# Taking the next tile's rows before a tile's last gelus, in a routed feed-forward stage on one NeuronCore

## The reference, cut to what matters

```
gate = softmax(xt @ Wg);  topv, topi = top_k(gate, 2);  scores[t, topi] = topv / (sum(topv) + 1e-6)
for e in range(8):
    h = gelu(xt @ W1[e] + b1[e])        # 256 -> 1024, exact gelu
    ye = h @ W2[e] + b2[e]              # 1024 -> 256
    out = out + ye * scores[:, e:e + 1]
```

## Time and profile before

| | us |
|---|---|
| median of 3 runs | 413.33 (411.07 to 414.03) |
| profiled execution | 412.78 |
| its span, first to last instruction | 410.8 |
| TensorE matmuls busy | 370.0 (90%) |
| VectorE busy | 259.3 (63%) |
| ScalarE busy | 255.5 (62%) |
| GpSimd busy | 179.0 (44%) |

### The profile page before, as it was taken

The page is one execution under the profiler, slowest core; times in us unless marked ns, Lnnn a source line. Parts: engine busy times, 40 slices in busy tenths (PEclk is TensorE's granted clock), DMA queues, the critical chain, the costliest instruction groups (busy, mean ns, idle before and its releaser), DMA issues.

```text
span 410.8 us, 8335 instructions
## 1 busy us (share of the span) xinstructions
PE 370.0 (90%) x2574; PEld 334.0 (81%) x2575; DVE 259.3 (63%) x651; ACT 255.5 (62%) x554; POOL 179.0 (44%) x227
## 2 busy tenths in 40 slices
PE   5989969999999997999989999999999999999950
PEld 4535557887888886999989899899999999899950
DVE  5868487796867876565467446784467754935530
ACT  2587556678658941756557566786567855765520
POOL 5800000002024544335655556675657546766553
PEclk9799999999999787999999999999999999999985
DMA  8810000000020781718224841569324624242342
GB/s 262 267 38 2 0 1 2 0 2 0 2 75 30 310 306 44 246 28 253 56 56 71 225 65 41 141 165 260 56 50 105 191 41 72 34 67 52 53 61 29
DMA packets 22964, 38.61 MB, mean 94 GB/s; under 512 B 2576, under 2 KB 17296, under 8 KB 22800
## 3 DMA queue, kind: packets, MB, share of 16 engines
q0 software_dynamic: 8032, 12.82, 18.7%
q1 hardware_dynamic: 14896, 25.41, 17.9%
HBM read 28.85 MB, written 9.37 MB: 93 GB/s over the span
## 4 chain that ended last, share of the span: by engine, by line
PE 39%; issue 7%; POOL 5%; DMA 5%; DVE 2%; ACT 2%; POOLq 1%; DVEq 0%; ACTq 0%
PE banks L1253 6%; PE banks L1577 6%; PE banks L1579 6%; PE banks L1581 6%; PE banks L1255 6%; PE banks L1254 6%; DMA xg<-xn_rows,idx_in 5%; PE banks L1554 3%; POOL xg L519 2%; POOL out_rows L565 2%; DVE y_out L1193 1%; ACT h_raw L812 0%; ACT h_hi L815 0%; ACT x_hi L802 0%; DVE w_lo L1211 0%
## 5 line engine op out<-in xcount | busy, mean ns | idle before, releaser
L812 ACT ACTIVATE h_raw<-banks,b1t 128x256 f32<-128x256 f32 (+1 forms) x136 | 68.0, 500 | 75.8 <-PE banks L1255 70.5
L1202 DVE TENSOR_TENSOR h_lo<-h_raw,h_hi 128x256 fp32r<-128x256 f32 (+1 forms) x136 | 59.8, 444 | 67.3 <-ACT h_hi L815 51.5
L565 POOL DMA_INDIRECT out_rows<-y_out,idx_out x36 | 68.6, 1907 | 42.8 <-DVE y_out L1193 37.0
L1253 PE MATMUL banks<-x_hi,w_hi 128*128 128x256 f32 (+1 forms) x272 | 79.6, 293 | 6.5 <-issue 3.9
L1577 PE MATMUL banks<-w_hi,h_hi 128*128 128x256 f32 x288 | 83.3, 289 | 1.0 <-DVE h_lo L1202 1.0
L1581 PE MATMUL banks<-w_hi,h_lo 128*128 128x256 f32 x288 | 81.4, 283 | 0.0
L1579 PE MATMUL banks<-w_lo,h_hi 128*128 128x256 f32 x288 | 81.4, 283 | 0.0
L1254 PE MATMUL banks<-x_lo,w_hi 128*128 128x256 f32 (+1 forms) x272 | 78.6, 289 | 0.0
L1255 PE MATMUL banks<-x_hi,w_lo 128*128 128x256 f32 (+1 forms) x272 | 78.6, 289 | 0.0
L519 POOL DMA_INDIRECT xg<-xn_rows,idx_in x57 | 58.0, 1017 | 27.8 <-POOL idx_in L514 16.2
L815 ACT ACTIVATE h_hi<-banks,b1t 128x256 fp32r<-128x256 f32 (+1 forms) x136 | 67.9, 499 | 0.0
(11 more groups left out here) (212 smaller groups left out, 676.1 us busy)
## 6 DMA issues: line engine op xcount, KB each, us to landing
w_raw<-in_w SPq DMA_DIRECT2D x16, 1024.0 KB
xn_rows<-xn SPq DMA_DIRECT2D x2, 1056.0 KB, 4.8
x<-in_x_tok SPq DMA_DIRECT2D x4, 512.0 KB, 5.6
out_rows<-x SPq DMA_DIRECT2D x1, 2048.0 KB, 9.3
b2b<-in_b SPq DMA_DIRECT2D x1, 1024.0 KB, 5.0
xg<-xn_rows,idx_in POOLq DMA_INDIRECT x57
out_rows<-y_out,idx_out POOLq DMA_INDIRECT x36, 3.9
out_rows<-x POOLq DMA_DIRECT2D x1, 384.0 KB, 3.2
```

What stands on the lines that cost most here:

```text
L565: pool.indirect_dma_start(out_d, bass.IndirectOffsetOnAxis(ap=idx_out[:, i:i + 1], axis=0), y_out[:, i, :], None, compute_op=ALU.add).then ...
L812: act.activation(h_raw[j % RING][:, 0:w], banks[:, j % RING, 0:w], ACT.Gelu, bias=bias)
L1202: dve.tensor_tensor(h_lo[:, j, 0:w], h_raw[j % RING][:, 0:w], h_hi[:, j, 0:w].bitcast(F32), ALU.subtract).then_inc(h_split, 1)
L1253: pe.matmul(out, a_hi, b_hi, start=start, stop=False)
```

## The change

On ScalarE, `x_high(t + 1)` goes from behind the last pair of gelus to ahead of it: behind the wait for the tile's last group of layer 1 and ahead of the wait for h_split. This holds in tiles with and without weight pieces. On VectorE, `x_low(t + 1)` goes from behind the last h_lo (and from ahead of the last w_lo, where there is one) to ahead of the waits for the last h_lo. No instruction is added or taken away.

```diff
@@ ScalarE, tile
                 for j in range(HJ):
                     act.wait_ge(l1_ready, t * HJ + (j + 1))
+                    if j == HJ - 1:
+
+                        x_high(t + 1)
 
                     act.wait_ge(h_split, t * HJ + (j + 1))
...
                         c = slice(j * PIECE, (j + 1) * PIECE)
-                        if j == HJ - 1:
-                            x_high(t + 1)
                         act.activation(w_hi[(e + 1) % 2][:, c], w_raw[(e + 1) % 2][:, c], ACT.Copy
                                        ).then_inc(whi_done, 1)
-                if not (split and e + 1 < E):
-                    x_high(t + 1)
@@ VectorE, tile
                 for j in range(HJ):
+                    if j == HJ - 1:
+                        x_low(t + 1)
                     dve.wait_ge(gelu_done, t * HJ + (j + 1 + RING))
                     dve.wait_ge(l2_done, t * HJ + (j + 1))
                     dve.tensor_tensor(h_lo[:, j, 0:w], h_raw[j % RING][:, 0:w], h_hi[:, j, 0:w].bitcast(F32),
...
                         c = slice(j * PIECE, (j + 1) * PIECE)
-                        if j == HJ - 1:
-                            x_low(t + 1)
                         dve.wait_ge(whi_done, HJ * (e + 1) + j + 1)
...
-                if not (split and e + 1 < E):
-                    x_low(t + 1)
```

## The result

The changed kernel takes 426.77 us (median of 4 runs, 425.92 to 427.34) against 412.72 us before (median of 4 runs): a ratio of 1.033, 95% interval 1.028 to 1.038. It is slower by 14 us. The forecast was 423.0 in a range of 416.5 to 427.0, slower with a chance of 0.85.

What follows compares the result with a forecast made beforehand. TensorE's order of instructions was taken as the bound. Ends inside an expert (2.8 us) and changes of expert (4.9 after tiles 2, 5, 9, 12; 2.5 after 6, 10, 13) gave +10.2 on 412.8: 423 us, range 416.5 to 427.

Steps and rivals of the forecast that it cites:

- The shift of the last h_lo: After a two-block tile without weight pieces, the last h_lo ends 1.50 us later, in tile 1 at 195.76 instead of 194.26.
- Inside an expert: Seven ends of two-block tiles: next start 0.65 us later each, 4.55 us together, of which 2.8 stay.
- At a change of expert: Next start 2.35 us after the last h_lo: 1.28 us later after tiles 2, 5, 9, 12, and 0.84 after 6, 10, 13.
- The clock: Rival: longer TensorE gaps lower the granted clock in the expert stage, some 8 us more, 431 us; chance 0.03.
- The rival of a gain: Starts after a change of expert wait for x_lo or the last w_lo; x_lo gains 2.5 us, 410.3 us; chance 0.06.
- the stalls at L1574: Sign: TensorE's layer 2 waits for h_lo grow from 3 places to about 15 and from 1.0 to 4 us.
- ScalarE's idle time before x_hi: Sign: in two-block tiles without weight pieces, ScalarE idles about 0.6 us before x_hi instead of before h_raw.
- The gaps ahead of L1250 at a change of expert: Sign: TensorE's gaps before first-layer matmuls at the seven changes of expert grow from 4.5 us to about 9.

Runs made afterwards that it cites:

- late_h_lo: Kernel before with one more VectorE subtraction of 128x256 into a spare tile ahead of every tile's last h_lo: 415.43 us, ratio 1.004.
- cover_before: Kernel before with each layer 1 group ahead of its layer 2 group on TensorE and the turn directly behind layer 1's last group: 414.35 us, ratio 1.002.
- swap_before: Kernel before with group j of layer 1 ahead of group j - 4 of layer 2 in TensorE's steady part: 411.57 us, ratio 0.993.
- bounds_before: Kernel before with the bounds of both experts of an outer loop turn loaded at its top on TensorE: 416.82 us, ratio 1.008.
- unrolled: swap_before with TensorE's expert loop written out and all eight experts' bounds loaded once ahead of tile 0: 421.95 us, ratio 1.017.
- cover_after: Changed kernel with each layer 1 group ahead of its layer 2 group on TensorE and the turn directly behind layer 1's last group: 419.19 us, ratio 1.012.

## Why the prediction was right, and where its sizes were off

**The shift of the last h_lo** was worked out at 1.50 us after a tile without weight pieces, 2.18 us behind the turn's end (193.58 to 195.76); it measured 2.17. The latency of 0.05 us and the 0.10 more of the first matmul were right too.

**Inside an expert** the term was 0.65 us an end, midway between 0.35 and 0.95. It measured the lower end: 0.87 us from h_lo to the start in all seven places, and tile 1 longer by 0.34. The loop's branches do wait for h_lo, but they take less time than the six matmuls. This term was sized too high by some 2 us.

**At a change of expert** the mechanism held and the size was too low. I charged a distance of 2.35 us everywhere, taken from tile 6, though tile 2 showed 2.57. The distances kept their own values, 2.61 after tile 2 and 2.82, 2.82 and 2.75 after 5, 9 and 12. So the shift of 1.5 us arrived in full: tiles 5, 9 and 12 are 1.46 to 1.48 us longer, not 1.28. At tiles 10 and 13 it was 0.87 and 0.59 for 0.84; the distance after tile 13 was 2.60 in the kernel before, where this one load took 0.51 us instead of 0.30, and 2.36 in the changed one. That the sequencer stands at the wait is shown by late_h_lo and by its own instructions in the trace.

The Trainium skill, in "Perfetto Trace Analysis", section on the Tensor Engine Instruction, says that the sequencer goes on to the next instruction once a matmul is in the wait queue. The traces here don't agree where the sequencer's next work is control: distances of 2.6 and 2.8 us with and without a stall speak against it, and so does the first branch instruction, which begins 0.07 us behind the last h_lo inside an expert too.

**The clock** had a chance of 0.03 as a rival, at 431. It was wrong to hold it so unlikely: two of the six gaps of 1.48 us or more were followed by a half clock. Tile 6 took 15.61 us with it, against 14.26 with a filled gap before it, so a fall is worth 1.3 us there; tile 3 was 2.4 us longer than before at 0.79 of the clock. Some 3 us of the 12.2 are the clock's, as an estimate. Without it the stage would have lost about 9 us where 10.2 were forecast: the two wrong sizes cancel in part, and the clock, which the sum had at nothing, took the time from there to 426.8. That this is still inside the range, by 0.2 us, is luck. Two smaller things that the profile was to show were wrong as well: the stalls at L1574 (see above), and ScalarE's idle time before x_hi, 1.25 us instead of 0.6, since the 0.6 that it had waited before h_raw is now part of it. The gaps ahead of L1250 at a change of expert grew to 10.3 us instead of about 9.

**The rival of a gain** was that the start waits for x_lo. It fell in the changed kernel itself, where x_lo ended 2.93 us ahead of tile 3, and again in cover_before.

**Open.** Why the gaps of 1.94 and 1.88 us left the clock alone while 1.73 didn't; and whether the sequencer would also be held at a wait whose count isn't computed in a register of the loop, as all of these are: no run tests that.

## What to carry to other kernels

What an engine does in the shadow of another's work is free only in that place. Here ScalarE's last two gelus ran while TensorE turned the next rows, and moving the step that needs those rows ahead of them made ScalarE wait out the turn, to bring x_lo 0.07 us sooner. Before moving a step ahead of others, ask what it waits for and who waits for the ones behind it; and look not only at the matmul that uses a result but at what the sequencer must still do behind that wait. If a loop's control takes 2.6 us, its last wait must be met 2.6 us ahead of the next start. Even then it is hidden only as far as the sequencer gets ahead of its engine, here some 2.1 us of matmuls; the rest must come out of the control itself.

## What the runs showed of the hardware that I had not expected

- TensorE's sequencer began its branches 0.07 us behind the last awaited h_lo, whether TensorE needed that h_lo at once or 1.28 us later, and never, at the end of a tile of two blocks, with more than 34 matmuls and weight loads still to start.
- The distance from the last h_lo to the first matmul of the next expert's tile came out the same to within 0.1 us for each place but one in ten kernels (the kernel before, the changed one and all but swap_before, cover_before, bounds_before and unrolled) whose times differed by up to 16 us: 2.54 to 2.62 after tile 2, 2.81 to 2.85 after tile 5. The exception is tile 13, 2.60 in the kernel before and 2.36 to 2.41 in the others.
- A load of an expert's bounds into TensorE's registers takes 0.75 us of the sequencer, 0.30 to 0.32 of it the load instruction itself in most places (0.50 and 0.51 in two of eight).
- Idle times of 1.4 to 2.1 us on TensorE were sometimes followed by 3 to 7 us at the 1.2 GHz level and sometimes not. Among the profiles here of kernels whose gaps at a change of expert reached 1.7 us or more, those not filled, each had one to three such falls that began in the stage, and cover_after, with gaps up to 1.6, had one. In the kernel before, with gaps up to 1.24, there was none in the stage.
